# Expert blocks: the up weights copied to a fixed buffer and held stationary, no transposes of the inner activation

## What is computed

```python
# layer 1: hidden 512                                            (stage 0 in the kernel)
h = gelu(t @ w1[e] + b1[e]) @ w2[e] + b2[e]
# layer 2: hidden 384, gated                                     (stage 1)
g = silu(einsum('td,xdh->txh', xf, wg)); u = einsum('td,xdh->txh', xf, wu)
eo = einsum('txh,xhd->txd', g * u, wd)
# layer 3: hidden 256, gated, one expert a token                 (stage 2)
a, g = split(xn @ up_w[e]); y = (a * silu(g)) @ down_w[e]
```

## Time and profile before

| | before |
|---|---|
| median of three runs | 1300.8 us |
| profiled execution | 1301.44 us |
| its span, first to last instruction | 1299.6 us |
| TensorE matmul busy | 1122.3 us (86%) |
| VectorE, ScalarE, POOL busy | 618.4, 513.6, 333.7 us |
| mean granted clock of TensorE | 0.876 |
| transposes of the inner activation, L1597 | 382, 62.2 us busy |
| up projections, L1573 and L1575 | 184 and 152 passes, 69.1 and 86.0 us busy |
| down projections, L1587 | 764 passes, 106.1 us busy |

### The profile page before, as it was taken

The page is one execution under the profiler, slowest core; times in us unless marked ns, Lnnn a source line. Parts: engine busy times, 40 slices in busy tenths (PEclk is TensorE's granted clock), DMA queues, the critical chain, the costliest instruction groups (busy, mean ns, idle before and its releaser), DMA issues.

```text
span 1299.6 us, 24883 instructions
## 1 busy us (share of the span) xinstructions
PE 1122.3 (86%) x9640; PEld 888.7 (68%) x9640; DVE 618.4 (48%) x1438; ACT 513.6 (40%) x1219; POOL 333.7 (26%) x312
## 2 busy tenths in 40 slices
PE   5988979988799997989796888879799979889894
PEld 4666766767577787878475777757577757867663
DVE  3644646447434336463564655446433336345332
ACT  2634515436255533323252232325244445154251
POOL 1021044210431533311302510130522353331322
PEclk9997969989799988978896788889799989688696
DMA  9100001000322240000000000000022230010122
GB/s 342 31 1 1 2 3 48 2 1 2 117 92 58 76 173 13 11 1 1 1 2 5 29 17 1 1 1 2 27 67 78 58 124 18 1 34 2 37 82 69
DMA packets 54033, 52.93 MB, mean 41 GB/s; under 512 B 6816, under 2 KB 49312, under 8 KB 53024
## 3 DMA queue, kind: packets, MB, share of 16 engines
q1 hardware_dynamic: 48800, 40.85, 9.6%
q0 software_dynamic: 5120, 10.50, 2.7%
HBM read 34.02 MB, written 17.30 MB: 39 GB/s over the span
## 4 chain that ended last, share of the span: by engine, by line
PE 77%; DVE 10%; POOL 5%; issue 4%; ACT 2%; DMA 1%; SPq 0%; POOLq 0%; DVEq 0%; ACTq 0%
PE bank L1587 7%; PE bank L1575 6%; PE bank L506 5%; PE bank L495 5%; PE bank L324 5%; PE bank L1573 5%; PE bank L287 4%; PE bank L304 3%; PE bank L870 3%; PE bank L1597 3%; PE bank L482 3%; POOL small L362 2%; PE bank L833 2%; PE bank L315 2%; PE bank L908 2%
## 5 line engine op out<-in xcount | busy, mean ns | idle before, releaser
L362 POOL TENSOR_TENSOR small<-small,neghalf 128x4 f32<-128x4 f32 x56 | 56.5, 1018 | 502.9 <-DVE small L384 325.8
L1587 PEld LDWEIGHTS bank<-wmoe,otx 128*128 128x128 f32 x764 | 103.5, 191 | 51.5 <-issue 39.9
L1260 POOL DMA_INDIRECT yg<-ybuf,posi x80 | 76.6, 957 | 216.7 <-DMA ybuf<-otx 189.7
L660 DVE TENSOR_REDUCE mx<-bank 128x8 f32<-128x512 f32 x128 | 88.1, 689 | 65.5 <-PE bank L482 62.8
L1587 PE MATMUL bank<-wmoe,otx 128*128 x764 | 106.1, 276 | 4.2 <-DVE otx L1689 1.8
L577 ACT ACTIVATE probsT<-bank 128x512 f32<-128x512 f32 x128 | 73.6, 597 | 87.3 <-PE bank L495 84.9
L495 PE MATMUL bank<-csb,probs 128*128 128x128 f32 x512 | 82.8, 294 | 22.9 <-ACT probs L581 22.9
L287 PE MATMUL bank<-warm_x,warm_w 128*128 128x224 bf16 x588 | 97.8, 276 | 0.0
L324 PE MATMUL bank<-csb,small 128*128 128x128 f32 x448 | 80.8, 347 | 18.6 <-POOL small L362 18.5
L1234 POOL DMA_INDIRECT xbuf<-rows,posi x80 | 78.3, 978 | 67.7 <-DVE ebi L1221 37.4
L324 PEld LDWEIGHTS bank<-csb,small 128*128 128x128 f32 x448 | 72.7, 250 | 25.0 <-POOL small L362 23.7
(11 more groups left out here) (271 smaller groups left out, 2145.3 us busy)
## 6 DMA issues: line engine op xcount, KB each, us to landing
ybuf<-otx SPq DMA_DIRECT2D x122, 64.0 KB
xblk<-xbuf SPq DMA_DIRECT2D x26, 256.0 KB
wmoe<-in_w_moe SPq DMA_DIRECT2D x3, 2048.0 KB, 10.2
wmoe<-in_w_moe SPq DMA_DIRECT2D x1, 3072.0 KB, 10.3
xbuf<-otx SPq DMA_DIRECT2D x2, 1472.0 KB, 19.9
wmoe<-in_w_moe SPq DMA_DIRECT2D x1, 1536.0 KB, 13.7
xbuf<-rows,posi POOLq DMA_INDIRECT x80, 2.2
yg<-ybuf,posi POOLq DMA_INDIRECT x80
```

The costliest lines, as they stand in the source:

```text
L362: g.tensor_tensor(s.col(1)[:, at:at + PC], s.col(0)[:, at:at + PC], neghalf[:, 0:PC], ALU.pow)\
L660: link(c, dve.tensor_reduce(s.mx[:, k % 2, :], by_head((s.SA, s.SB)[k % 2][:, :]), AX.X, ALU.max))
L1260: nc.gpsimd.indirect_dma_start(yg[:, p % 2, k, i, :], None, ybuf[g].ap(), bass.IndirectOffsetOnAxis(ap=posi[g][:, j:j + 1], axis=0)).then_ ...
L1587: mm = pe.matmul(YB[:, 0:P], aT[:, na % 3, ch * P:(ch + 1) * P], wmoe[:, bass.ds(e * (H * P) + at, P)], start=(ch == 0), stop=(ch == H - 1))
```

## The change

The up projection is turned round: the weights are the stationary operand and the tokens stream, so that its result has hidden units on the partitions and tokens along the row, as the down projection wants it. The transposes `turn`, the bank pair `AT` and ScalarE's copies out of it are gone; three pairs of banks now rotate for the up results. The stationary weights come from a fixed buffer `w_up` of two halves (laid into `qx`, which the attention part uses), into which VectorE copies the expert's 512, 768 or 512 columns from `wmoe` two blocks ahead (`weights`). VectorE therefore reads the expert number in all stages. In stage 0 VectorE adds the bias, broadcast along the tokens, on the way out of PSUM, and ScalarE does GELU in one instruction of 512 columns. In stages 1 and 2 VectorE's product writes `aT` itself. The down projection follows its up by two rounds instead of three. `moe_sp` is unchanged.

```diff
             def up(n):
-                expert[n] = e = pe.value_load(ebi[g][0:1, b:b + 1], min_val=0, max_val=NE - 1)
+                expert[n] = pe.value_load(ebi[g][0:1, b:b + 1], min_val=0, max_val=NE - 1)
                 pe.wait_ge(m["blockT_taken"], na + 1)
-                if na >= 2:
-                    pe.wait_ge(m["up_taken"], na - 1)
...
+                pe.wait_ge(m["up_weights"], na + 1)
+                if na >= 3:
+                    pe.wait_ge(m["act"], na - 2)
+                U = UP[na % 3]
+                for ch in range(H):
+                    for half in range(1 if l == 0 else 2):
+                        w = w_up[:, na % 2, (ch if l == 0 else 2 * ch + half) * P:]
+                        mm = pe.matmul(U[half][:, ch * P:(ch + 1) * P], w[:, 0:P], xTs[:, na % 3, :],
+                                       start=True, stop=True)
                 mm.then_inc(m["up"], 1)
...
-            for it in range(-2, N + 2):
+            for it in range(-2, N + 1):
                 if it + 2 < N:
                     take(it + 2)
                 if 0 <= it + 1 < N:
                     up(it + 1)
-                if 0 <= it - 2:
-                    down(it - 2)
-                if 0 <= it < N:
-                    turn(it)
+                if 0 <= it - 1:
+                    down(it - 1)
...
             def act(n):
...
+                a.wait_ge(m["up_taken"], na + 1)
+                if na >= 3:
+                    a.wait_ge(m["down"], na - 2)
+                a.activation(aT[:, na % 3, :], us[:, na % 2, :], ACT.Gelu_apprx_tanh).then_inc(m["act"], 1)
...
+            def weights(n):
+                na, g, b = place(l, n)
+                if b == 0:
+                    dve.wait_ge(prepared, NG * l + g + 1)
+                expert[n] = dve.value_load(ebi[g][0:1, b:b + 1], min_val=0, max_val=NE - 1)
+                if na >= 2:
+                    dve.wait_ge(m["up"], na - 1)
+                dve.tensor_copy(w_up[:, na % 2, 0:wide], wmoe[:, bass.ds(expert[n] * wide, wide)])\
+                   .then_inc(m["up_weights"], 1)
...
             def product(n):
...
+                    bias = vsb[:, bass.ds(expert[n] * 4 + vplace["b1"][0], 4)].unsqueeze(2).to_broadcast([P, 4, P])
+                    dve.tensor_tensor(us[:, na % 2, :].rearrange("p (c n) -> p c n", n=P),
+                                      U[0][:, :].rearrange("p (c n) -> p c n", n=P), bias, ALU.add)\
+                       .then_inc(m["up_taken"], 1)
                 else:
...
+                    dve.tensor_tensor(aT[:, na % 3, 0:H * P], sg[:, na % 2, 0:H * P], U[1][:, 0:H * P], ALU.mult)\
+                       .then_inc(m["act"], 1)
...
+            for it in range(-2, N + 1):
+                if it + 2 < N:
+                    weights(it + 2)
+                if 0 <= it + 1 < N:
                     product(it + 1)
-                if 0 <= it - 2:
-                    down(it - 2)
+                if 0 <= it - 1:
+                    down(it - 1)
```

More of the change, by code:

```diff
@@ L89 @@
                  "skip_added", "route_done", "moe_scaled", "moe_ready", "moeT"]
-MOE_SIGNALS = ["blockT", "blockT_taken", "up", "gated", "up_taken", "hiddenT", "act", "down", "down_taken"]
+MOE_SIGNALS = ["blockT", "blockT_taken", "up_weights", "up", "gated", "up_taken", "act", "down", "down_taken"]
 def build(nc, fin, iin, consts, vecs, weights, out):
@@ L200, in build @@
         xTs = sb("xTs", [P, 3, P])
-        XT, YB, AT, UP = banks[0], banks[1], banks[2:4], banks[4:8]
+        XT, YB = banks[0], banks[1]
+        UP = [banks[2 + 2 * i:4 + 2 * i] for i in range(3)]
         class Stream:
@@ L1622, in gate @@
                 a.wait_ge(m["up"], na + 1)
[L1623 to L1630, removed]
+                a.wait_ge(m["act"], na - 1)
+                a.activation(sg[:, na % 2, 0:H * P], UP[na % 3][0][:, 0:H * P], ACT.Silu).then_inc(m["gated"], 1)
             def act(n):
                 na, g, b = place(l, n)
[L1634 to L1646, removed]
+                a.wait_ge(m["up_taken"], na + 1)
+                if na >= 3:
+                    a.wait_ge(m["down"], na - 2)
+                a.activation(aT[:, na % 3, :], us[:, na % 2, :], ACT.Gelu_apprx_tanh).then_inc(m["act"], 1)
             for it in range(-2, N):
@@ L1650, in moe_act @@
                     take(it + 2)
[L1651 to L1654, removed]
+                if 0 <= it + 1 < N:
+                    if l == 0:
+                        act(it + 1)
+                    else:
+                        gate(it + 1)
         def moe_dve(l):
@@ L1658, in moe_dve @@
             N, H = NG * NBLK[l], CHUNKS[l]
+            wide = (4, 6, 4)[l] * P
+            expert = {}
+            def weights(n):
[7 more added lines that the diff above has]
+                   .then_inc(m["up_weights"], 1)
@@ L1666, in product @@
                 else:
                     dve.wait_ge(m["gated"], na + 1 - NG * NBLK[0])
[L1668 to L1674, removed]
@@ L1675, in product @@
-                i.then_inc(m["up_taken"], 1)
+                    dve.wait_ge(m["down"], na - 2)
+                    dve.tensor_tensor(aT[:, na % 3, 0:H * P], sg[:, na % 2, 0:H * P], U[1][:, 0:H * P], ALU.mult)\
+                       .then_inc(m["act"], 1)
             def down(n):
                 na, g, b = place(l, n)
[L1679 to L1682, removed]
+                e = expert.pop(n)
@@ L1690, in down @@
                 i.then_inc(m["down_taken"], 1)
+            dve.wait_ge(dma_w["moe"], 32 * (l + 1))
             if l == 0:
                 dve.wait_ge(dma_w["b2"], 16 * NE)
-            for it in range(-1, N + 2):
-                if it + 1 < N:
+            for it in range(-2, N + 1):
+                if it + 2 < N:
+                    weights(it + 2)
+                if 0 <= it + 1 < N:
                     product(it + 1)
-                if 0 <= it - 2:
-                    down(it - 2)
+                if 0 <= it - 1:
+                    down(it - 1)
         def moe_sp(l, behind=None):
```

16 lines of the change are left out of this document (6 added, 10 removed).

## The result

The changed kernel took 1268.7 us (median of four runs, 1264.5 to 1276.1) against 1301.7 for the kernel before, measured beside it: a ratio of 0.976, with a 95% interval of 0.973 to 0.979. The forecast was 1268. The profiled execution took 1267.3 us with a span of 1265.5, so 34.1 us less than the span of before.

The account below looks back on a forecast made before the run. After the change a two-block loop through VectorE and TensorE's queue was to bound all stages, at 2.00, 2.15 and 1.80 us a block. Savings of 19.8 + 11.3 + 1.7 = 33 us from 1301.4 gave 1268, range 1262 to 1275.

Parts of the forecast that it names:

- The reading of before: Before the change: stage 1 runs at the array's rate, 2.40 us; the instruction stream ahead of the array holds stages 0 and 2.
- the floors given: Array time per block before the change: 2.29, 2.40 and 1.62 us in stages 0, 1 and 2.
- Rival A: The array sets all three stages after the change: 1.88, 2.10, 1.43 us a block, saving 51 us, so 1250; chance 0.19.
- the very loop that the prediction named: Two-block round trip, VectorE's take through TensorE's expert-number reading to the next up projection: 1.97, 2.12, 1.76 us a block.
- The reading's length: TensorE's queue: reading the expert number stays in the way from VectorE's take to the next up, 1.32 us in stage 2.
- The surcharge: 0.03 to 0.05 us added to each stage's loop, because the sum fell 0.05 short of stage 2's block before.
- rival B's first way: VectorE becomes the bound, copying one column a cycle: blocks 2.13, 2.26, 1.86 us, time 1280 to 1286; chance 0.12.
- VectorE's rounds: VectorE's time from take to take after the change, durations summed: 1.86, 1.86, 1.59 us, below blocks of 2.00, 2.15, 1.80.
- The cover in stage 0: Slack of VectorE's 1.86 us round under stage 0's 2.00 us block: 0.14 us.
- rival B's second way: VectorE's weight copies wait on POOL, one in four at 0.44 us: 13 us, 8 behind the cover, 1276 to 1281; chance 0.08.
- Rival C: Slower: VectorE's queue doesn't read ahead, blocks 2.42, 2.54, 2.14 us, 13 us more, 1314; chance 0.08.
- Starts and ends: Each stage's start about 0.8 us later for the first weights, one end round of 1.87 us gone: 0 ± 3 us altogether.

Follow-up runs that it names:

- the early reading: Kernel before, with only TensorE's reading of the expert number moved ahead of the down matmuls' wait, transposes and streamed weights kept: 1283.3 us, 0.986 of before.
- the version with the early reading: Changed kernel with TensorE's reading of the expert number moved ahead of the down matmuls' wait: 1259.1 us, 0.9675 of before; once more, 1258.7 us.
- the doubled reading: Changed kernel with TensorE reading the expert number twice in a row ahead of each up projection: 1301.1 us, 1.001 of before.

## Why the prediction held, step by step

**What bounds.** The reading of before held: the early reading brought stages 0 and 2 down to the floors given and left stage 1 where it was. Rival A's floors for after, 1.88, 2.10 and 1.43, were right for stages 0 and 1 (1.90, 2.12; a pass holds 0.112 us, and 17 and 19 of the 0.11 that the sum was written with would be 1.87 and 2.09); A's result, 1250, didn't come because of the very loop that the prediction named.

**The three blocks.** Forecast 2.00, 2.15 and 1.80; measured 2.03, 2.21 and 1.72. The sum, 33 us against 31, agreed better than its terms: 19.8, 11.3 and 1.7 us were forecast, 18.7, 8.5 and 4.1 came. That the time came out within 1 us of 1268 is luck in part: the blocks gave 2 us less than forecast, and the untouched code around the stages was 2.8 us shorter than in the profile of before, while between the two profiles of the changed kernel it differs by as much (997.4 and 1000.0 us). Two terms were mis-sized.

- *The reading's length.* It went in at the 0.30 us of one row of before. Here are its rows in stage 0 before, in the first and the middle stage after, and in stage 0 of the version with the early reading (ns min/median/max):

```profile
L1565 PEldq TENSOR_LOAD <-ebi x41: 296/300/312, 362.9 to 459.8; - x41
```

```profile
L1568 PEldq TENSOR_LOAD <-ebi x42: 297/392/454, 358.9 to 442.1; - x42
L1568 PEldq TENSOR_LOAD <-ebi x41: 296/333/507, 918.1 to 1006.5; - x41
```

```profile
L1568 PEldq TENSOR_LOAD <-ebi x41: 297/301/500, 360.9 to 438.6; - x41
```

  In stage 0 it grew from a median of 0.30 to 0.39: 0.05 us a block, and the block is 0.03 over the forecast. In stage 1 the loop by itself, by the estimate above, is the 2.13 that was forecast within 0.02. What was missing is what happens when loop and array tie: a longer reading or a held copy delays the loop, and the array can't make the time up. Some six in ten of stage 1's blocks took 2.12 us, the others up to 2.7, on average 2.21; with the reading moved, 39 of 41 took 2.12, and the other two were those with held copies. A tie deserved more than the 0.03 that was added.
- *The surcharge.* In stage 2, 0.04 was added to a loop of 1.76 since the same sum had fallen short by 0.05 before. The loop there turned out as 1.73, and the surcharge was wrong.

**The copies.** 0.43 and 0.56 us, the lower ends that were taken (median 427 and 560 ns), and 0.76 us behind the take in stage 0, as forecast. In stages 1 and 2 they start earlier, at a median of 0.43 and 0.50 us behind it, since the queue reads the number under the product that waits. The slow price of rival B's first way is out.

**VectorE's rounds.** 1.86, 1.86 and 1.59 were too long, by 0.15 in stage 0: durations were added where starts had to be. The cover in stage 0 was 0.3 and not 0.14.

**Waits on POOL, rival B's second way.** The mechanism is there, its reach wasn't: not one copy in four but four of 122 were held for more than a quarter of a microsecond (0.26 to 1.3 us), all by TENSOR_TENSOR and none by the indirect transfers. The price is 0.6 to 3 us in the changed kernel and up to 3.5 with the early reading, against 8 to 13. The row that it was taken from says less than was read from it: before, the instruction of 545 ns at 168.46 us stood under POOL's TENSOR_SCALAR work as did that of 989 ns at 166.85. The Trainium skill, SBUF — State Buffer, section "Who interferes with whom", says that whoever issues first keeps the shared port pair for the whole instruction. The copy at 427.06 agrees: it began 0.86 us behind POOL's multiplication and ended 0.29 us behind it. The copy at 425.09 above, drawn 0.02 us ahead of POOL's instruction, was held all the same, so which of two came first can't be read from such rows to that degree; and the copies under gathers and scatters, mostly of unchanged length, show that the rule doesn't hold for POOL's time in those as the profile draws it.

**ScalarE and the waits for weights.** GELU took 0.63 us (0.62 forecast) and stayed hidden. In stage 0 TensorE waited for copied weights once, behind the copy that POOL had held.

**Rival C** needed a queue that doesn't read ahead; it does.

**Starts and ends.** Forecast at 0 ± 3 us in all. The start of stage 0, for the earlier trace rows:

```profile
348.18 0.18 DVE L1224 TENSOR_SCALAR ebi<-ebf 128x23 int32<-128x23 f32 x1
...
349.90 0.43 DVE L1648 COPY qx<-wmoe 128x512 f32 x1 [1.55 <-issue]
...
350.48 2.05 PE L1577 MATMUL bank<-xTs,qx 128*128 128x128 f32 x8 [2.23 <-DVE qx L1648]
```

```profile
L1644 DVEq EVENT_SEMAPHORE  x1: 659/659/659, 348.2 to 348.2; - x1
```

From the end of the routing (348.36) to the first up projection it is 2.12 us, before 0.37: 1.75 more, where 0.8 was forecast. The number is read later than in a running stage, since nothing else covers its wait: VectorE's queue waits for the routing until 348.85 (L1644), the load then takes 0.55 us, and 1.55 us in all pass ahead of the first copy. The round saved at the end is worth 1.87 by the rows of before. The three stages whole lost 31.4 us and their blocks 31.2, so the cancelling held, with larger parts on both sides than forecast.

**The granted clock** in the middle of all three stages stayed at 1.00, the 2.4 GHz level, so no part of the blocks' change comes from it (windows as in the earlier trace rows; before it was 1.00 in all three too):

```profile
358.00:443.00 85.00, 84.32 (x713) 80.24 (x711) 57.95 (x126) 33.16 (x85) 30.62 (x29) 1.00 0.29 81
917.00:1008.00 91.00, 90.20 (x785) 87.80 (x784) 56.61 (x125) 31.75 (x83) 33.44 (x30) 1.00 0.26 75
1198.00:1240.00 42.00, 40.10 (x319) 36.39 (x318) 25.70 (x73) 16.14 (x49) 9.99 (x10) 1.00 0.30 85
```

## What to carry to other kernels

Taking work off a busy engine brings its full price only down to the next loop: here 41 us of transposes became 31, because a register read of 0.66 us stood once in a loop over two blocks; moving that read one step earlier in the queue gave 11.5 us more. Look for loops that pass through a queue's register reads and waits, and for any two limits within a few hundredths of each other, since a tie costs more than either. For the round of an engine that runs back to back, add start-to-start distances and not durations.

## What the runs showed of the hardware

- Reading one number from SBUF into a register of TensorE, with its steps, costs some 0.66 us of its queue's time (2 × 0.33 from the doubled reading; 403.2 to 403.9 in the queue's rows), though the load itself has medians of 0.30 to 0.39.
- The same load's median went from 0.30 to 0.39 us in stage 0 after the change and back to 0.30 when it was moved. What lengthens it wasn't tested.
- On VectorE, an instruction without a wait starts some 0.08 us before the one ahead of it ends (0.43 and 0.42 us copies 0.34 apart).
- A copy of VectorE's that met POOL's TENSOR_TENSOR work ended 0.29 us behind it and took 1.35 us in place of 0.43; 51 copies that met its indirect transfers had a median excess of nothing.
- Stretches of untouched code between the stages differ by up to 5.7 us from kernel to kernel and execution to execution, roughly in step with their mean granted clock (173.8 us at 0.82, 169.1 at 0.84): as much as one experiment's effect.
